# A six-layer local-attention kernel: queries' halves first, the mask as four products, the final sum per tile, and late setup work made inside the first stage

## What is computed

```python
x = x + self_attention(layernorm(x))               # 16 heads of 8 channels
x = x + cross_attention(layernorm(x), ctx, mask)   # 16 heads of 64, padding mask
x = x + ffn(layernorm(x))                          # the local stage, 6 layers:
# for each layer i, with x the stage's own running value:
    q, k, v = split(shift_tokens(x) @ Wqkv[i])     # 16 heads of 64
    q, k = rotary(l2norm(q) * qs), rotary(l2norm(k) * ks)
    sim = 8 * q @ k.T, where(k > q or q > k + 32) -> masked
    x = softmax(sim) @ v @ Wo[i] + x
    a, gate = split(layernorm(shift_tokens(x)) @ W1[i] + b1[i])
    x = (a * gelu(gate)) @ W2[i] + b2[i] + x
```

## Time and profile before

| | |
|---|---|
| time, median of 3 runs | 3785.52 us (3785.45 to 3789.49) |
| the profiled execution's own time | 3781.1 us |
| its span | 3779.3 us |
| granted clock of PE, mean | 0.992 |
| busy, share of the span | PE 96%, PEld 70%, ACT 77%, DVE 74%, POOL 68% |

### The profile page before, as it was taken

How to read it: one execution, slowest core, us unless ns; L and a number is a source line. 1 busy time by engine, 2 the same in 40 slices (tenths; PEclk the granted TensorE clock), 3 DMA queues, 4 the chain that set the end, 5 groups by cost and what they waited for, 6 DMA issues and landing times. The chain is left out here.

```text
span 3779.3 us, 124845 instructions
## 1 busy us (share of the span) xinstructions
PE 3614.2 (96%) x50565; PEld 2635.3 (70%) x50757; DVE 2785.0 (74%) x5266; ACT 2905.5 (77%) x5539; POOL 2588.6 (68%) x4812
## 2 busy tenths in 40 slices
PE   6989997999999999999999999999999999999996
PEld 4778874677677777776777767777667777777765
DVE  5834446788777877777777777778777787777874
ACT  4756664788888888888888888888888888888885
POOL 4622225777777777777777777777777777777773
PEclk9999999999999999999999999999999999999998
DMA  3000000000000000000000000000000000000001
GB/s 94 3 10 9 8 5 19 17 10 10 10 19 21 18 10 10 10 23 24 10 10 10 15 25 18 10 9 10 24 24 10 9 10 16 14 10 9 10 10 28
DMA packets 145046, 59.08 MB, mean 16 GB/s; under 512 B 116954, under 2 KB 139231, under 8 KB 144479
## 3 DMA queue, kind: packets, MB, share of 16 engines
q1 hardware_dynamic: 144478, 51.08, 5.5%
HBM read 23.95 MB, written 2.10 MB: 7 GB/s over the span
## 5 line engine op out<-in xcount | busy, mean ns | idle before, releaser
L1341 DVE TENSOR_TENSOR R<-bank,tables 128x1024 f32<-128x1024 f32 x768 | 919.5, 1218 | 243.0 <-ACT sq L1247 242.7
L1043 PE MATMUL bank<-WA,xcT 128*128 128x512 f32 x1536 | 694.5, 595 | 4.6 <-ACT xcT L1221 2.7
L1247 ACT ACTIVATE sq<-bank 128x512 f32<-128x512 f32 x768 | 459.3, 598 | 159.9 <-PE bank L1043 159.9
L1446 POOL TENSOR_TENSOR R<-R 128x512 f32<-128x512 f32 x384 | 481.1, 1275 | 0.0
L1043 PEld LDWEIGHTS bank<-WA,xcT 128*128 128x128 f32 x1536 | 277.2, 190 | 284.1 <-issue 190.8
L1221 ACT ACTIVATE qT<-bank 128x512 f32<-128x512 f32 x384 | 229.7, 598 | 286.9 <-PE bank L1125 286.9
L1356 DVE TENSOR_REDUCE ss<-sq 128x16 f32<-128x1024 f32 x384 | 444.3, 1198 | 4.4 <-ACT sq L1247 4.2
L1095 PE MATMUL bank<-WV,xcT 128*64 128x512 f32 x1536 | 414.2, 618 | 0.0
L1460 POOL TENSOR_TENSOR P<-P,rn 128x512 f32<-128x512 f32 x384 | 404.9, 1055 | 0.6 <-DVE P L1384 0.6
L1466 POOL TENSOR_TENSOR P<-P,inv_sum 128x512 f32<-128x512 f32 x384 | 403.1, 1050 | 0.8 <-DVE inv_sum L1396 0.8
L1187 PE MATMUL bank<-WO,OT 128*128 128x128 f32 x3072 | 396.8, 283 | 0.0
(11 more groups left out here) (157 smaller groups left out, 7818.2 us busy)
## 6 DMA issues: line engine op xcount, KB each, us to landing
WA<-in_wqkv SPq DMA_DIRECT2D x24, 256.0 KB, 2.9
ystat<-Y SPq DMA_DIRECT2D x192, 32.0 KB
ystat<-Y SPq DMA_DIRECT2D x384, 15.8 KB
ys<-Y SPq DMA_DIRECT2D x192, 32.0 KB
ys<-Y SPq DMA_DIRECT2D x384, 15.8 KB
WV<-in_wqkv SPq DMA_DIRECT2D x6, 512.0 KB, 3.7
WO<-in_wo SPq DMA_DIRECT2D x6, 512.0 KB, 4.4
X<-in_x SPq DMA_DIRECT2D x4, 512.0 KB, 5.1
```

What stands on the lines that cost most here:

```text
L1043: mm(b[QK_BANK[n, half]][:, :], m.xsT[:, k % 2, :], cols[:, half, :, :], start=True, stop=True)\
L1247: nc.scalar.activation(by_half[:, half, :, :], b[QK_BANK[n, half]][:, :].rearrange("p (h d) -> p h d", d=32), ACT.Square)\
L1341: tt(both, src.unsqueeze(1).to_broadcast([128, 2, 16, 32]), tab.unsqueeze(2).to_broadcast([128, 2, 16, 32]), ALU.mult).then_inc(s.rotated, 1)
L1446: tt(m.R[:, KEYS, 0, at], m.R[:, KEYS, 0, at], m.R[:, KEYS, 1, at], ALU.add).then_inc(s.k_added, 1)
```

## The change

1. **Queries' halves first.** The projections come as queries 0, queries 1, keys 1, keys 0. ACT squares in that order. DVE does rotary of queries 0 and of queries 1 one after the other, then the sum of the queries' squares, then `statistics`, then the sum of the keys' squares; the rest of its turn stays as it was. The waits on `s.qk`, `s.squared` and `s.summed` follow the new numbering.
2. **Mask in four products.** The causal mask is written by four products of 64x64 by 64x512, one for each quarter, in place of two of 128x128 by 128x512.
3. **Final sum per tile.** `finish` is gone. In the last layer, DVE adds `Y` to `X` tile by tile, right after `ff_added`, and SP stores four tiles at a time (256 KB), one turn later at the earliest.
4. **Late setup work in the first stage.** `setup` ends without the wait on `loads` and without L243 to L251. DVE does this work in turns 10 to 22 of the first stage, in 13 pieces, between `input_statistics` and `added`: the two casts, a quarter of `maskb` four times, one of the eight table products eight times. The wait for the loads stands in turn 10.

```diff
@@ setup, DVE
-            dve.wait_ge(late, 16 * len(loads))
-            dve.tensor_copy(m.identb[:, :], m.ident[:, :])
-            dve.tensor_copy(m.causalb[:, :], m.causal)
-            dve.tensor_scalar(m.maskb[:, :], m.mask8[:, :].bitcast(U8), MASKED, None, ALU.mult)
-            for n in range(2):
-                for frm in range(2):
-
-                    for s, to in ((0, frm), (1, 1 - frm)):
-                        at = slice(to * half, (to + 1) * half)
-                        dve.tensor_tensor(m.tables[:, :, n, frm, s, :], m.scales[:, n, s, :, at],
-                                          m.rot[:, n, s, at].unsqueeze(1).to_broadcast([128, DEPTH, half]), ALU.mult)
@@ self_attention, DVE
+            def constants_made(i):
+                if i == 0:
+                    dve.wait_ge(m.late_in, m.late_count)
+                    dve.tensor_copy(m.identb[:, :], m.ident[:, :])
+                    dve.tensor_copy(m.causalb[:, :], m.causal)
+                elif 1 <= i < 5:
+                    words = slice((i - 1) * 256, i * 256)
+                    dve.tensor_scalar(m.maskb[:, (i - 1) * 1024:i * 1024], m.mask8[:, words].bitcast(U8), MASKED, None,
+                                      ALU.mult)
+                elif 5 <= i < 13:
...
+                    tt(m.tables[:, :, n, frm, s, :], m.scales[:, n, s, :, at],
+                       m.rot[:, n, s, at].unsqueeze(1).to_broadcast([128, DEPTH, HD // 2]), ALU.mult)
             for i in range(N + 5):
                 input_statistics(i)
+                constants_made(i - 10)
                 added(i - 4)
@@ local, SP
+            def store(n):
+                if n > 0 and n % STORED == 0:
+                    part = slice(n - STORED, n)
+                    sp.wait_ge(s.final, n)
+                    sp.dma_start(out[:, part, :], m.X[:, part, :]).then_inc(s.stored, 16)
             def turn(i, k, l):
                 layer_input(i + 1, k + 1, l)
                 ff_input(i - 5, k - 5)
+                store(i - LAST - (N - TILES))
@@ local, PE
                     heads_in(t, k, QUERIES, 0)
+                    if filling(t, 7):
+                        at_least(pe, s.q_copied, 2 * t - 1)
+                    heads_in(t, k, QUERIES, 1)
                     at_least(pe, s.y, t - 6)
                     if filling(t, 7):
                         at_least(pe, s.rotated, 4 * t)
                     heads_in(t, k, KEYS, 1)
-                    if filling(t, 7):
-                        at_least(pe, s.q_copied, 2 * t - 1)
-                    heads_in(t, k, QUERIES, 1)
                     heads_in(t, k, KEYS, 0)
@@ scores
-                    for a in range(2):
-                        mm(S_BANK[a][:, :], m.identb[:, :], m.causalb[:, :], start=True, stop=False)
+                    crossed = ((0, 0), (1, 1), (0, 1), (1, 0))
+                    for a, bb in crossed:
+                        half = slice(64 * a, 64 * a + 64)
+                        mm(S_BANK[a][64 * bb:64 * bb + 64, :], m.identb[half, half], m.causalb[half, :],
+                           start=True, stop=False)
@@ local, ACT
                 squares(i, QUERIES, 0, 0)
-                squares(i, KEYS, 1, 1)
-                squares(i, QUERIES, 1, 2)
+                squares(i, QUERIES, 1, 1)
+                squares(i, KEYS, 1, 2)
                 squares(i, KEYS, 0, 3)
@@ local, DVE
                     tt(y, y, FF_OUT[:, 0:128], ALU.add).then_inc(s.y, 1)
+                    if layer(t) == DEPTH - 1:
+                        x = tile_of(m.X, t)
+                        dve.wait_ge(s.y, t + 1)
+                        tt(x, x, y, ALU.add).then_inc(s.final, 1)
...
                 rotary(i, QUERIES, 0, 1)
+                rotary(i, QUERIES, 1, 2)
+                squares_summed(i, k, QUERIES)
                 statistics(i - 5, k - 5)
-                squares_summed(i, k, QUERIES)
                 squares_summed(i, k, KEYS)
-                rotary(i, QUERIES, 1, 3)
                 seeded(i, k)
```

More of the change, by code:

```diff
@@ L170, in build @@
         m.x_in = [sem(f"x_in_{n}") for n in range(4)]
+        m.late_in = sem("late_in")
         m.cross_w = sem("cross_weights")
@@ L178, in build @@
         local(nc, sem, m)
-        finish(nc, sem, m)
 def setup(nc, sem, m):
-    early, late, zeroed, tril_in = sem("setup_early"), sem("setup_late"), sem("setup_zeroed"), sem("setup_tril_in")
+    early, zeroed, tril_in = sem("setup_early"), sem("setup_zeroed"), sem("setup_tril_in")
     made, turned, copied = sem("setup_made"), sem("setup_turned"), sem("setup_copied")
@@ L195, in setup @@
             loads.append((m.b1col[0:rows, side, c, :], m.b1T[side * FF + at:side * FF + at + rows, :]))
+    m.late_count = 16 * (len(loads) + 6)
     half = HD // 2
@@ L218, in _ @@
             for dst, src in loads:
-                sp.dma_start(dst, src).then_inc(late, 16)
+                sp.dma_start(dst, src).then_inc(m.late_in, 16)
         @block.gpsimd
@@ L267, in _ @@
             act.activation(m.wqk[:, :], m.bank[1][:, 0:128], ACT.Copy)
-def finish(nc, sem, m):
-    summed, stored = sem("finish_summed"), sem("finish_stored")
-    parts = 4
-    n = TILES // parts
-    out = m.out.rearrange("(t b) s d -> (b s) t d", b=2)
-    with nc.Block() as block:
-        @block.vector
-        def _(dve):
-            for c in range(parts):
-                part = slice(c * n, (c + 1) * n)
-                dve.tensor_tensor(m.X[:, part, :], m.X[:, part, :], m.Y[:, part, :], ALU.add).then_inc(summed, 1)
-        @block.sync
-        def _(sp):
-            for c in range(parts):
-                part = slice(c * n, (c + 1) * n)
-                sp.wait_ge(summed, c + 1)
-                sp.dma_start(out[:, part, :], m.X[:, part, :]).then_inc(stored, 16)
-            sp.wait_ge(stored, 16 * parts)
 def load_input_weights(sp, m, l, par, c):
@@ L554, in less_maximum @@
                        mx.unsqueeze(3).to_broadcast([128, 4, 4, SEQ]), ALU.subtract).then_inc(s.less, 1)
+            def constants_made(i):
[8 more added lines that the diff above has]
+                elif 5 <= i < 13:
+                    n, frm, s = (i - 5) // 4, (i - 5) // 2 % 2, (i - 5) % 2
+                    to = frm if s == 0 else 1 - frm
+                    at = slice(to * HD // 2, (to + 1) * HD // 2)
+                    tt(m.tables[:, :, n, frm, s, :], m.scales[:, n, s, :, at],
+                       m.rot[:, n, s, at].unsqueeze(1).to_broadcast([128, DEPTH, HD // 2]), ALU.mult)
             for i in range(N + 5):
                 input_statistics(i)
+                constants_made(i - 10)
                 added(i - 4)
@@ L889 @@
 QUERIES, KEYS = 0, 1
+STORED = 4
 FIRST, LAST = 0, 7
@@ L943, in local @@
     s.ff, s.gelu, s.h, s.w2, s.y = sem("local_ff"), sem("local_gelu"), sem("local_h"), sem("local_w2"), sem("local_y")
+    s.final, s.stored = sem("local_final"), sem("local_stored")
     held = sem("local_held")
@@ L950, in layer @@
         return t // TILES
+    out = m.out.rearrange("(t b) s d -> (b s) t d", b=2)
     with nc.Block() as block:
@@ L1007, in _ @@
                     load_value_weights(sp, m, l + 1)
-            for i in range(N, N + 5):
+            for i in range(N, N + LAST + 1):
                 turn(i, i % 2, DEPTH)
+            sp.wait_ge(s.stored, 16 * (TILES // STORED))
         @block.tensor
@@ L1102, in scores @@
                     pe.wait_ge(s.k_copied, 2 * t + 2)
-                    for a in range(2):
-                        mm(S_BANK[a][:, :], m.identb[:, :], m.causalb[:, :], start=True, stop=False)
+                    crossed = ((0, 0), (1, 1), (0, 1), (1, 0))
[3 more added lines that the diff above has]
+                           start=True, stop=False)
                     for hp in range(PAIRS):
-                        for a, bb in ((0, 0), (1, 1), (0, 1), (1, 0)):
+                        for a, bb in crossed:
                             head, at = slice(64 * a, 64 * a + 64), hp * 128 + bb * 64
@@ L1243, in squares @@
                     act.wait_ge(s.qk, 4 * t + at + 1)
-                    if at < 2:
+                    if at % 2 == 0:
                         at_least(act, s.summed, 2 * t - 1 + n)
@@ L1354, in squares_summed @@
                 if inside(t, N):
-                    dve.wait_ge(s.squared, 4 * t + 3 + n)
+                    dve.wait_ge(s.squared, 4 * t + 2 + 2 * n)
                     nc.vector.tensor_reduce(m.ss[:, k % 2, 16 * n:16 * n + 16],
```

## The result

The changed kernel takes 3670.96 us in the median of 4 runs (3669.16 to 3673.49), against 3786.34 for the kernel before in 4 runs (3785.45 to 3789.49). The ratio is 0.9694 with a 95% interval from 0.9678 to 0.9711: 115 us faster. The prediction had 99.5 us less and 3686 us, with a range from 3672 to 3720. The mean granted clock is the same as before (0.991 against 0.992), so the clock has no part in it. So the question for the experiments is which gain was left out, and whether the terms that looked right were right for the reasons given.

What follows compares the result with a forecast made beforehand. PE, busy 96% of the span, bounds the kernel, with DVE tied before the queries' transposes. Gains 59.5 + 21.6 + 4.5 + 7.4 + 6.5 = 99.5 us take 3785.5 to 3686 us; range 3672 to 3720.

Steps and rivals of the forecast that it cites:

- The mask (59.5 us): Local stage, mask to first score product: four products save 0.31 us a turn over 192 turns, 59.5 us.
- The order (21.6 + 4.5 us): Before the transposes of the queries: 21.6 us of PE stalls on DVE's rotary removed, plus 4.5 in quiet turns.
- What is late next: After the reorder, POOL to ACT's query copies is tightest, covered by less than 0.1 us; DVE keeps 0.4 us.
- rivals 2 and 4: POOL-ACT chain becomes the bound: 3705 to 3744 us (12 in 100), or slower than before (3 in 100).
- rival 4: Slower than before through the POOL-ACT chain, deciding from 0.52 us beyond the slack in every turn; 3 in 100.
- Setup (7.4 us): Start: first stage begins 9.4 us earlier, 2 us of late DVE work shows; 7.4 us gained (4.5 to 9.4).
- The end (6.5 us): Last sum of `Y` to the end: 10.8 us becomes 4.3, gaining 6.5 us (5 to 7).

Runs made afterwards that it cites:

- the other shape: The changed kernel with the mask in four products of 128x64 by 128x512: 3727.48 us, 56.5 above the changed kernel.

## Why the prediction came out as it did

- **The mask (59.5 us).** Right in mechanism and size: values to first score product went from 1.547 to 1.249 us, 0.298 a turn and 57 us, where 0.31 and 59.5 were taken. The step that failed is beside it: "from the first weight load of the mask to the first score product" was taken as the whole of what the mask's shape changes. The scores behind it gain 0.060 us more from first to last product, 11.5 us, since their first weights are loaded under the mask. The cross stage's row had such products behind their own shape, but the 0.16 us between its 0.93 and 1.09 was read as the price of the change of shape behind them alone. By the starts 0.13 of it is that change (0.149 against 0.021 us to the next product) and the rest the beginning (0.943 against 0.907 us from first to last). With this term the sum is 111 us and the time 3674.5, inside the range. The runs with the order alone, the mask alone and the other shape show it. The other 4.4 of the 115.4 us are smaller terms: 0.1 in the local stage, 1.9 at the setup, 1.3 at the end and 3.4 between the profiled executions and the medians, against 2.3 lost in the cross stage and the drain.
- **The order (21.6 + 4.5 us).** Right. The trace gives 28.3 us for these waits, the run with the order alone 35 by the medians (30.7 by the profiled turns with the filling; the first turn went from 13.53 to 11.44 us there, to 11.65 in the changed kernel, which the prediction left out). That the mask's gain alone "would end at DVE" was right to the nanosecond.
- **What is late next.** The chain over POOL and ACT was seen in the right place, and its slack mis-sized: "0.05 behind", "by less than 0.1 us", where more than 1.2 us were free. Two numbers in it were too high. POOL's three instructions took 1.85 us after the statistics in the earlier trace rows because POOL had other work in front (it began them at 2014.39, right behind L1466); now it stands ready, and they end 1.5 us after (2009.67 to 2011.22). And a late first copy of the queries harms nobody: PE waits only for the second one and for what follows, with waits of ACT between. So rivals 2 and 4 were given too much of the 100; where rival 4 decides was right in kind, as the kernel with the statistics behind the keys shows.
- **Setup (7.4 us).** 9.2 us at the start, as worked out (23.20 against 22.97 foretold), and 9.3 with the first stage. The pieces lengthen five turns of the first stage by 0.15 us each, 0.7 in all, not 2: the quarter of the mask takes 0.66 us, but the waits of the turn take most of it. That the first stage as a whole is not longer is scatter, as the table's note says: in five other kernels with this work it takes 2 us more.
- **The end (6.5 us).** 7.8: the small store lands in 2.4 us (median of 8), the load of the same size that stood for it in 2.9, and 3.5 was taken.
- **The range.** Its good end, worked out as 3676, took the mask's best case and hidden setup work as the only good surprises, and the range was opened to 3672. It was short by 1 us. Which side of 3672 the time fell on lies within the scatter; the missing 11.5 us does not.

## What to carry to other kernels

When an instruction is released 0.05 us before the bounding engine reaches it, the engine has no idle time to show and yet a gain on that engine is worth nothing: look at the distance from the releaser's end to the start, and move the releaser first. Count a change of tile shape on TensorE by its neighbours on both sides, for what follows can begin faster too (0.06 us a turn here, 11.5 us in all). A chain that a profile shows as long because its engine was busy gets shorter when it is moved to where the engine stands ready; measure its slack by moving it one place further.

## What the hardware showed that I had not expected

- The score products, from first to last of 64: 0.883 us behind products of their own tile shape, 0.943 behind those of another (eight kernels and four).
- A DVE sum of 128x128 with both operands in on-chip memory: 0.29 us alone, 0.95 in the median beside a busy POOL; with one operand in a PSUM bank 0.29 always. It seems to work the other way too: while DVE made a quarter of the mask (0.66 us) in the first stage, POOL's instruction on one column took 0.57 us instead of 0.22, in all four cases. No run was made to show the cause. The first of the four:

```profile
75.62 0.66 DVE L531 TENSOR_SCALAR maskb<-mask 128x1024 bf16<-128x1024 uint8 x1
75.79 0.57 POOL L555 TENSOR_SCALAR vare<-mv_in 128x1 f32<-128x1 f32 x1 [0.93 <-DVE mv_in L491]
```

- One wait of 2.67 us in a turn cost PE more than itself: right behind it, from 2003.2 to 2006.6 us, the granted clock was at the lower of its two levels, and twelve products took 2.73 us in place of 1.49.
